# A selective-scan stage on one core: the per-chunk front work placed three steps earlier, and exponentials four states ahead instead of three

## The chip, the core and the metric

The kernel runs on 1 core of one Trainium2 chip. The metric is the device time of one execution in microseconds (us). All of it is one launch; nothing is computed on the host.

The core has five engines with a queue each, and each works its queue strictly in the order of the program: PE (TensorE, matmuls), DVE (VectorE), ACT (ScalarE), POOL (GpSimd) and SP (SyncE, which here only issues DMAs). An instruction that waits for a semaphore holds up everything behind it on its engine.

## What is computed

The reference is four layers on x of shape (8, 128, 64, 64), each of the form `x = x + layer(group_norm(x))`. The change touches layer 0 alone, so only that is shown, cut to what matters (D = 64, DI = 128, N = 16 states, L = 4096 positions, 8 images):

```python
x_id, x_hw = x[:, :64], x[:, 64:]                 # two halves of the channels
t  = (tokens(x_id) @ expand_w) @ concat_w + concat_b
xs, z = split(layer_norm(t) @ in_w + in_b)        # 2 x 128
xc = silu(conv1d_3(xs))                           # 3 causal taps
dt, Bm, Cm = softplus(xc @ ... ), xc @ ..., xc @ ...
h_t = exp(dt_t * A) * h_(t-1) + dt_t * Bm_t * xc_t     # for each of 16 states
y_t = sum_n h_t[n] * Cm_t[n] + xc_t * D
x_id_out = t + (y * silu(z)) @ out_w + out_b
hw = conv3x3(x_hw)
x = x + relu(concat(x_id_out, hw))
```

Layers 1 to 3 (a row and column propagation, a gated convolution, a deformable convolution) follow and are the same in both kernels.

## The kernel before, in words

Layer 0 is the function `layer0`. Its work is cut into 64 **chunks** of 512 positions: 8 chunks (`NCH`) of each of 8 images. Channels lie on the 128 partitions, positions along the free dimension, so every tile is 128x512. Image 0 is unrolled, images 1 to 7 are one hardware loop.

A chunk g has 16 **steps** n = 0 to 15, one for each state. Each engine runs its own list of steps, and semaphores tie the lists together:

- DVE (L1007, L1017, L999): *product* n+1 (dt*x times the B row, in PSUM), then *scan* n (the recurrence over 512 positions). So a chunk begins with products 0 and 1 and then scan 0. After scan 2 comes *gated* of the chunk before: it reads the finished sum `pY` and multiplies it by silu(z).
- POOL (L979): *weigh* n, h times the C row, after scan n, into one of eight buffers `hc`.
- PE: at step n first *spread* n+3 (L884; it broadcasts the B row of that state into one of four PSUM banks `pB`, after scan n-1; from n = 13 on these are spreads 0, 1, 2 of the next chunk), then the *sums* (L873; sum k adds the weighed state k into `pY` after weigh k). `SUM_AT` says which at which step: 11 at step 13, 12 at step 14, 13 at step 15, and, as `LATE_SUM_AT`, 14 and 15 at steps 0 and 1 of the next chunk. Then the 3x3 convolution's matmuls that `CONV_AT` gives to the step (`taps`: first the direct one, L890, which waits until `fin` of the chunk before has been read out of `pO`; then two low ones, L893, on partitions 64 to 127; then three pairs, L896).
- ACT (L940): *decay*, the exponential exp(dt*A) of the state `LEAD` ahead of n; at step 3 also the *direct term* (L928, xc*D into `pY`, which must wait for gated and comes before sum 0), at step 4 the *result* (L933, relu into `fin`), at step 13 the statistics.

Beside that, each chunk has **front work**, which is done for a chunk ahead: norm, halo, centre, variance, deviation, normalise (which make `un`), taps and gate input (the causal conv and z), silu (xc and silu(z), with a table load before and after), projections, dt argument, round B and C (whose last write is `c_out`), log, rest of B and C, softplus (two instructions), dt, dt * x. Three tables `PE_AT`, `ACT_AT` and `POOL_AT` put each at the end of a step. On POOL a chunk has 16 weighs, one result addition (L984, step 6) and six front instructions, 23 in all. SP loads inputs and the broadcast C rows; its own list isn't changed.

A matmul on fp32 data shows in the trace as two records ("x2"); a spread is one. Two matmuls that use different partition halves (a low convolution tap beside centre or variance, tap 2 beside the gate input) run side by side.

Of the kernel before, what the change touches and what calls it, by code (L numbers as in the profile page):

```python
# [24 lines left out]
B, H, W = 8, 64, 64  # L25
HW = H * W
CH = 512
NCH = HW // CH
ROWS = CH // W
HALF = 64  # L30
NS = 16
# [8 lines left out]
def after(eng, sem, k, lag=0):  # L40


    eng.wait_ge(sem, k + (1 + CREDIT - lag))
# [456 lines left out]
def layer0(nc, G, x_dram, x1_dram, c_dram):  # L500
# [3 lines left out]
    NDA = 8  # L504
    NHC = 8
    NB = 4
    LEAD = 3
    KEEP = G.KEEP
    with ExitStack() as ctx:
        def sb(name, shape, dt=F32):  # L510
            return ctx.enter_context(nc.sbuf_tensor(name, shape, dt))
# [24 lines left out]
        rest = sb("m_rest", [P, CH])  # L536
# [3 lines left out]
        dt = sb("m_dtv", [P, 2, CH])  # L540
# [21 lines left out]
        def sem(name):  # L562
# [20 lines left out]
        s.passed = ctx.enter_context(nc.semaphore("m_waits_passed"))  # L583


        PE_AT = {0: ["tap 0"], 1: ["tap 1"], 2: ["tap 2", "gate input"], 5: ["project B, C", "project dt"], 8: ["centre"],
                 10: ["variance"]}
        ACT_AT = {1: ["norm", "halo"], 3: ["silu"], 6: ["dt argument", "round B, C"], 8: ["log", "pad"], 9: ["centre"],
                  11: ["deviation"]}
        POOL_AT = {7: ["rest of B, C"], 9: ["softplus"], 10: ["dt"], 11: ["dt * x"], 13: ["normalise"]}  # L590
        TWO_AHEAD = ("norm", "halo", "centre", "variance", "deviation", "normalise")
        CONV_AT = {7: 1, 8: 1, 10: 1, 11: 1, 13: 1, 15: 1}
        SUM_AT = {4: (0, 1), 6: (2, 3), 7: (4, 5), 8: (6,), 9: (7,), 10: (8,), 11: (9,), 12: (10,), 13: (11,), 14: (12,),
                  15: (13,)}
        LATE_SUM_AT = {0: 14, 1: 15}
# [117 lines left out]
        def front_pool(g, b, c, what):  # L713
            pool, par = nc.gpsimd, c % 2
            if what == "normalise":
                after(pool, s.rstd, g)
                after(pool, s.z, g, 2)
                after(pool, s.cv, g, 2)
                after(pool, s.halo, g, 1)
                pool.tensor_tensor(un[:, par, 2:2 + CH], tc[:], sq[:], ALU.mult).then_inc(s.u, 1)  # L720
            if what == "rest of B, C":
                after(pool, s.c_out, g)
                after(pool, s.HC, NS * (g - 1) + 7)
                pool.tensor_tensor(bcs[32:64, par, :], bcf[32:64, par, :], bcs[32:64, par, :].bitcast(F32),
                                   ALU.subtract).then_inc(s.blo, 1)
                after(pool, s.blo, g)
            if what == "softplus":
                after(pool, s.r1, g)
                pool.tensor_tensor(rest[:], ea[:], rest[:], ALU.subtract).then_inc(s.r2, 1)
                after(pool, s.r2, g)  # L730
                after(pool, s.ln, g)
                pool.tensor_tensor(rest[:], rest[:], ln[:], ALU.add).then_inc(s.r3, 1)
            if what == "dt":
                after(pool, s.r3, g)
                after(pool, s.xb, g)
                pool.tensor_tensor(dt[:, par, :], dt[:, par, :], rest[:], ALU.add).then_inc(s.dt, 1)  # L736
            if what == "dt * x":
                after(pool, s.dt, g)
                after(pool, s.xc, g)
                after(pool, s.U, 16 * g - 16, 1)  # L740
                pool.tensor_tensor(dtx[:, par, :], dt[:, par, :], xc[:, par, :], ALU.mult).then_inc(s.dtx, 1)

        def program(eng, at, chunk, front, finish, before=lambda: None):

            def parts(n, one_ahead, two_ahead):
                for what in at.get(n, ()):
                    where = two_ahead if what in TWO_AHEAD else one_ahead
                    if where:  # L750
                        front(*where, what)

            def image(b, last):
                def place(c):

                    if c >= NCH:
                        return b * NCH + c, (b + 1) % B, c - NCH
                    return b * NCH + c, b, c
                for c in range(NCH):
                    prev = place(c - 1) if c else (b * NCH - 1, b - 1, NCH - 1) if last else None  # L760
                    chunk(b * NCH + c, b, c, prev, lambda n: parts(n, place(c + 1), place(c + 2)))
            for n in range(NS):
                parts(n, None, (0, 0, 0))
            for n in range(NS):
                parts(n, (0, 0, 0), (1, 0, 1))
            before()
            image(0, False)
            with eng.Fori(1, B) as b:
                image(b, True)
            finish(B * NCH - 1, B - 1, NCH - 1)  # L770

        with nc.Block() as block:
            @block.sync
            def _(sp):
# [82 lines left out]
                after(sp, s.sum, NS * G_LAST + NS - 1)  # L857
                after(sp, s.dA, NS * B * NCH + LEAD - 1)
                for b in range(KEEP, G.NI):
# [8 lines left out]
            def _(pe):  # L868
                def sum_state(g, n):
                    after(pe, s.HC, NS * g + n)  # L870
                    if n == 0:
                        after(pe, s.dterm, g)
                    pe.matmul(pY[:], G.ident, hc[:, n % NHC, :], start=False, stop=(n == NS - 1),  # L873
                              skip_group_check=True).then_inc(s.sum, 1)
# [5 lines left out]
                def spread_B(g, n, par):  # L880
                    if n == 0:
                        after(pe, s.blo, g)
                    after(pe, s.S, NS * g + n, NB)
                    pe.matmul(pB[:, n % NB, :], T.pick[:, n:n + 1].to_broadcast([P, P]), bcs[:, par, :],  # L884
                              start=True, stop=True).then_inc(s.B, 1)
# [12 lines left out]
                def chunk(g, b, c, prev, parts_ahead):  # L898
                    tap = taps(g, c)
                    for n in range(NS):  # L900
# [8 lines left out]
                        for k in SUM_AT.get(n, ()):  # L909
                            sum_state(g, k)  # L910
                        for _ in range(CONV_AT.get(n, 0)):
                            next(tap)
                        parts_ahead(n)

                def finish(g, b, c):
                    for k in LATE_SUM_AT.values():
                        sum_state(g, k)
                    project_out(g, c)
                pe.matmul(pY[:], G.ident, G.small[:, 0:CH], start=True, stop=True).then_inc(s.border, 1)
                program(pe, PE_AT, chunk, front_pe, finish, lambda: [spread_B(0, n, 0) for n in range(3)])  # L920

            @block.scalar
            def _(act):
# [28 lines left out]
                def chunk(g, b, c, prev, parts_ahead):  # L952
                    for n in range(NS):
                        if n < NS - LEAD:
                            decay(g, n + LEAD, c % 2)
                        else:
                            decay(g + 1, n + LEAD - NS, 1 - c % 2)
                        if n == 3:
# [7 lines left out]
                def finish(g, b, c):  # L966
                    result(g, b, c)
                    statistics(g, b, c)
                program(act, ACT_AT, chunk, front_act, finish, lambda: [decay(0, n, 0) for n in range(LEAD)])

            @block.gpsimd
            def _(pool):
# [13 lines left out]
                def chunk(g, b, c, prev, parts_ahead):  # L986
                    for n in range(NS):
# [3 lines left out]
                        parts_ahead(n)  # L991
                program(pool, POOL_AT, chunk, front_pool, result)

# [865 lines left out]
```

## Time and profile before

| | us |
|---|---|
| median of 3 runs (7603.76 to 7632.84) | 7619.43 |
| the profiled execution's span | 7648.3 |
| layer 0: first to last *gated*, 64 of them | 141.0 to 2121.3 |
| PE busy, whole span | 5717.8 (75%) |
| DVE busy | 5490.3 (72%) |
| POOL busy | 4111.0 (54%) |
| ACT busy | 3409.0 (45%) |

The profiled execution took 29 us (0.4%) more than the median. Layer 0 is 26% of the span. Shares over the whole span mix four layers with different limits, so layer 0 is read chunk by chunk, in the timeline of each engine. In that timeline one row is an instruction or a run of equal ones; the start of the next row is the truer measure of what an instruction costs its engine, since the recorded lengths overlap by some hundredths of a microsecond.

### The profile page before, as it was taken

The numbers are of one execution on the slowest core, as the hardware profiler recorded it, in microseconds if no ns is written. First come the engines' busy times: TensorE is split into PE (matmuls) and PEld (weight loads), VectorE is DVE, ScalarE is ACT, GpSimd is POOL, SyncE is SP. The second block draws the span as 40 slices with busy tenths as digits, with TensorE's granted clock in tenths as the row PEclk, the third lists the DMA queues.
The fourth block names the chain that finished last, engine by engine and source line by source line (L and its number), as shares of the span: only waits on it lengthen the run. The fifth ranks groups of instructions, "written<-read, shape, count | busy, mean of one in ns | idle before, by whom it ended". The sixth has DMA issues, their size and how long they took to land. (4 is left out here: it accounts for less than half of the span.)

```text
span 7648.3 us, 89071 instructions
## 1 busy us (share of the span) xinstructions
PE 5717.8 (75%) x21147; PEld 3269.1 (43%) x21147; DVE 5490.3 (72%) x12779; ACT 3409.0 (45%) x7221; POOL 4111.0 (54%) x3871
## 2 busy tenths in 40 slices
PE   5999999999989999999865565655656565565442
PEld 2444444444478888888532222322223232232111
DVE  6999999999967777778565666556566665665556
ACT  4888888888855211111233333333333333333333
POOL 4999999999910001000055555655556565565663
PEclk9999999999999999999987676877778777687665
DMA  5445444444420000000156555555555665555567
GB/s 193 170 179 180 167 169 172 170 168 167 168 87 3 3 0 23 0 0 0 42 164 198 164 184 178 168 183 168 180 180 172 193 184 183 178 176 179 178 182 265
DMA packets 306397, 1093.60 MB, mean 143 GB/s; under 512 B 56560, under 2 KB 58639, under 8 KB 264604
## 3 DMA queue, kind: packets, MB, share of 16 engines
q0 software_dynamic: 187440, 625.23, 27.1%
q1 hardware_dynamic: 118516, 464.08, 17.0%
q14 instruction: 359, 2.94, 0.1%
q8 instruction: 82, 1.34, 0.1%
HBM read 997.72 MB, written 91.37 MB: 142 GB/s over the span
## 5 line engine op out<-in xcount | busy, mean ns | idle before, releaser
L1281 POOL DMA_INDIRECT d_ring<-corner_table,d_idx_now x2304 | 2212.2, 960 | 1635.9 <-issue 950.2
L1481 PE MATMUL d_ps_s<-small,d_mix 128*128 128x128 f32 x2304 | 489.6, 350 | 1544.2 <-DVE d_mix L1653 1010.5
L979 POOL TENSOR_TENSOR X<-X 128x512 f32<-128x512 f32 x1024 | 1289.7, 1277 | 168.3 <-DVE X L1017 150.9
L1481 PEld LDWEIGHTS d_ps_s<-small,d_mix 128*128 128x128 f32 x2304 | 327.8, 176 | 2071.0 <-issue 1089.5
L1653 DVE SCALAR_TENSOR_TENSOR d_acc<-d_ring,d_w_now,d_mix 128x128 f32<-128x128 f32 x2304 | 660.9, 354 | 694.3 <-ACT d_mix L1327 321.5
L1017 DVE TENSOR_TENSOR_SCAN X<-X,m_pB 128x512 f32<-128x512 f32 x896 | 1132.4, 1269 | 0.0
L873 PE MATMUL m_pY<-X,small 128*128 128x512 f32 x2048 | 1040.4, 605 | 90.3 <-POOL X L979 90.2
L277 PE MATMUL prop_ps<-prop_parts,prop_w_hi 128*128 128x480 f32 (+4 forms) x4536 | 1099.8, 387 | 4.6 <-DVE prop_parts L286 4.6
L1327 ACT ACTIVATE d_mix<-d_ring,d_w_now 128x128 f32<-128x128 f32 x2304 | 732.3, 390 | 719.1 <-DMA d_ring<-corner_table,d_idx_now 659.1
L277 PEld LDWEIGHTS prop_ps<-prop_parts,prop_w_hi 128*128 128x128 f32 x4536 | 816.0, 188 | 133.4 <-DVE prop_parts L286 5.4
L1411 PE MATMUL d_ps_out<-d_samp,d_dcn_w 128*128 128x512 f32 x1152 | 832.0, 815 | 7.9 <-ACT X L1314 5.8
L1007 DVE TENSOR_TENSOR m_pB<-m_dtx,m_pB 128x512 f32<-128x512 f32 x1024 | 693.0, 678 | 92.2 <-PE m_pB L884 69.3
L884 PE MATMUL m_pB<-m_bcs,m_pick 128*128 128x512 f32 x1027 | 758.9, 739 | 0.1
L940 ACT ACTIVATE X<-m_dtv,m_A 128x512 f32<-128x512 f32 x1027 | 688.5, 713 | 96.3 <-POOL m_dtv L736 74.7
L225 ACT ACTIVATE prop_sum<-prop_ps 128x256 f32<-128x256 f32 x504 | 194.5, 386 | 1169.4 <-PE prop_ps L277 1169.4
L1653 DVE SCALAR_TENSOR_TENSOR d_mix<-d_ring,d_w_now,d_acc 128x128 f32<-128x128 f32 x2304 | 646.8, 340 | 85.1 <-remote 45.7
L1653 DVE SCALAR_TENSOR_TENSOR d_acc<-d_ring,d_w_now,d_acc 128x128 f32<-128x128 f32 x2304 | 649.5, 348 | 43.5 <-DVE d_acc L1653 26.4
L272 PEld LDWEIGHTS prop_ps<-prop_parts,prop_w_lo 128*128 128x128 f32 x4536 | 598.3, 189 | 51.8 <-issue 9.8
L272 PE MATMUL prop_ps<-prop_parts,prop_w_lo 128*128 128x240 f32 (+4 forms) x4536 | 604.1, 277 | 16.4 <-POOL prop_w_lo L200 9.6
L873 PEld LDWEIGHTS m_pY<-X,small 128*128 128x128 f32 x2048 | 363.7, 188 | 469.8 <-POOL X L979 281.6
L1440 PE MATMUL l_ps_a<-l_xn,l_w 128*128 128x512 f32 x896 | 462.9, 648 | 24.1 <-DVE l_gate L1541 24.1
L200 POOL TENSOR_TENSOR prop_w_lo<-prop_raw,prop_w_hi 128x1152 fp32r<-128x1152 f32 x4 | 10.6, 2648 | 793.1 <-ACT prop_w_hi L218 793.1
(231 smaller groups left out, 7744.8 us busy)
## 6 DMA issues: line engine op xcount, KB each, us to landing
X<-c_scratch SPq DMA_DIRECT2D x256, 1024.0 KB, 4.9
d_ring<-corner_table,d_idx_now POOLq DMA_INDIRECT x2304
corner_table<-d_tT SPq DMA_DIRECT2D x120, 256.0 KB
X<-in_x SPq DMA_DIRECT2D x8, 2048.0 KB, 15.2
m_res<-in_x SPq DMA_DIRECT2D x64, 256.0 KB, 4.6
x_scratch<-m_res SPq DMA_DIRECT2D x64, 256.0 KB, 2.1
x_scratch<-X SPq DMA_DIRECT2D x8, 2048.0 KB
b_x<-x_scratch POOLq DMA_DIRECT2D x16, 1024.0 KB, 11.7
```

What stands on the lines that cost most here:

```text
L272: pe.matmul(ps[s][:, 1, a:b, :], w_lo[:, d % 2, k * P:(k + 1) * P], parts[s][:, 0, a + k - MID:b + k - MID, :], start=(k == MID), stop=Fal ...
L277: mm = pe.matmul(ps[s][:, :, a:b, :], w_hi[:, d % 2, k * P:(k + 1) * P], parts[s][:, :, a + k - MID:b + k - MID, :], start=False, stop=(k ...
L873: pe.matmul(pY[:], G.ident, hc[:, n % NHC, :], start=False, stop=(n == NS - 1), skip_group_check=True).then_inc(s.sum, 1)
L884: pe.matmul(pB[:, n % NB, :], T.pick[:, n:n + 1].to_broadcast([P, P]), bcs[:, par, :], start=True, stop=True).then_inc(s.B, 1)
L979: pool.tensor_tensor(hc[:, n % NHC, :], h[:, n, :], Cb[:, n, :], ALU.mult).then_inc(s.HC, 1)
L1007: dve.tensor_tensor(pB[:, n % NB, :], dtx[:, c % 2, :], pB[:, n % NB, :], ALU.mult).then_inc(s.U, 1)
L1017: dve.tensor_tensor_scan(h[:, n, :], dA[:, n % NDA, :], pB[:, n % NB, :], T.zero[:, 0:1] if c == 0 else h[:, n, CH - 1:CH], ALU.mult, ALU. ...
L1281: pool.indirect_dma_start(out=ring[:, m % RING, :], out_offset=None, in_=flat, in_offset=bass.IndirectOffsetOnAxis(ap=idx_now[:, c % 2, m: ...
L1327: r0 = act.activation(R[:, k % 3, t, :], ring[:, m % RING, 0:P], ACT.Copy, scale=w_now[:, c % 2, 4 * m:4 * m + 1])
L1411: pe.matmul(ps_out[:], dcn_w[:, k, :], samp[:, k % 3, :], start=(k == 0), stop=(k == TAPS - 1)).then_inc(s_dcn, 1)
L1481: turned = pe.transpose(ps_s[k % 3][:, t, :], R[:, k % 3, t, :], G.ident)
L1653: mixed = dve.scalar_tensor_tensor(R[:, k % 3, t, :] if corner == 3 else acc[:, t, :], ring[:, m % RING, corner * P:(corner + 1) * P], w_n ...
```

## The change

The front work moves three steps earlier on all engines: what stood at step n of a chunk for the next chunk stands at n-3 now, and what falls off the beginning goes to the end of the chunk before, one chunk further ahead (three tables with the distance written beside each name, `AHEAD = 3` passes before the first chunk instead of two). "pad" stays at step 8. The convolution's direct tap and first low tap move to step 5, the others to 7, 9, 10 and 12. `LEAD` is 4. Sums, the result additions, the direct term and the statistics stay where they were.

```diff
-    LEAD = 3
+    LEAD = 4
-        PE_AT = {0: ["tap 0"], 1: ["tap 1"], 2: ["tap 2", "gate input"], 5: ["project B, C", "project dt"], 8: ["centre"],
-                 10: ["variance"]}
-        ACT_AT = {1: ["norm", "halo"], 3: ["silu"], 6: ["dt argument", "round B, C"], 8: ["log", "pad"], 9: ["centre"],
-                  11: ["deviation"]}
-        POOL_AT = {7: ["rest of B, C"], 9: ["softplus"], 10: ["dt"], 11: ["dt * x"], 13: ["normalise"]}
-        TWO_AHEAD = ("norm", "halo", "centre", "variance", "deviation", "normalise")
-        CONV_AT = {7: 1, 8: 1, 10: 1, 11: 1, 13: 1, 15: 1}
+        PE_AT = {2: [("project B, C", 1), ("project dt", 1)], 5: [("centre", 2)], 7: [("variance", 2)],
+                 13: [("tap 0", 2)], 14: [("tap 1", 2)], 15: [("tap 2", 2), ("gate input", 2)]}
+        ACT_AT = {0: [("silu", 1)], 3: [("dt argument", 1), ("round B, C", 1)], 5: [("log", 1)], 6: [("centre", 2)],
+                  8: [("pad", 1), ("deviation", 2)], 14: [("norm", 3), ("halo", 3)]}
+        POOL_AT = {4: [("rest of B, C", 1)], 6: [("softplus", 1)], 7: [("dt", 1)], 8: [("dt * x", 1)],
+                   10: [("normalise", 2)]}
+        AHEAD = 3
+        CONV_AT = {5: 2, 7: 1, 9: 1, 10: 1, 12: 1}
...
-                after(pool, s.HC, NS * (g - 1) + 7)
+                after(pool, s.HC, NS * (g - 1) + 4)
...
-            for n in range(NS):
-                parts(n, None, (0, 0, 0))
-            for n in range(NS):
-                parts(n, (0, 0, 0), (1, 0, 1))
+            for g in range(-AHEAD, 0):
+                for n in range(NS):
+                    parts(n, lambda ahead: (g + ahead, 0, g + ahead) if g + ahead >= 0 else None)
```

**POOL, a chunk of image 0.** L979 is weigh, L984 the result, L724 rest of B and C, L729 and L732 softplus, L736 dt, L741 dt * x, L720 normalise. Before, from the nine weighs 14, 15, 0 to 6 on:

```order
L979 TENSOR_TENSOR X<-X 128x512 x9
L984 TENSOR_TENSOR m_res<-m_res,m_fin 128x512
L979 TENSOR_TENSOR X<-X 128x512
L724 TENSOR_TENSOR m_bcs<-m_bcf,m_bcs 32x512
L979 TENSOR_TENSOR X<-X 128x512 x2
L729 TENSOR_TENSOR m_rest<-m_ea,m_rest 128x512
L732 TENSOR_TENSOR m_rest<-m_rest,m_ln 128x512
L979 TENSOR_TENSOR X<-X 128x512
L736 TENSOR_TENSOR m_dtv<-m_dtv,m_rest 128x512
L979 TENSOR_TENSOR X<-X 128x512
L741 TENSOR_TENSOR m_dtx<-m_dtv,m_xc 128x512
L979 TENSOR_TENSOR X<-X 128x512 x2
```

The same place now, from the ten weighs 11 to 15 and 0 to 4 on (front lines have moved by one line number):

```order
L979 TENSOR_TENSOR X<-X 128x512 x10
L725 TENSOR_TENSOR m_bcs<-m_bcf,m_bcs 32x512
L979 TENSOR_TENSOR X<-X 128x512 x2
L984 TENSOR_TENSOR m_res<-m_res,m_fin 128x512
L730 TENSOR_TENSOR m_rest<-m_ea,m_rest 128x512
L733 TENSOR_TENSOR m_rest<-m_rest,m_ln 128x512
L979 TENSOR_TENSOR X<-X 128x512
L737 TENSOR_TENSOR m_dtv<-m_dtv,m_rest 128x512
L979 TENSOR_TENSOR X<-X 128x512
L742 TENSOR_TENSOR m_dtx<-m_dtv,m_xc 128x512
L979 TENSOR_TENSOR X<-X 128x512 x2
L721 TENSOR_TENSOR m_un<-m_tc,m_sq 128x512
```

All seven instructions that aren't weighs stand between weigh 4 and weigh 11 now; before they stood between weigh 6 and weigh 14.

**PE, from step 13 to step 1 of the next chunk**, image 0. L873 is a sum, L884 a spread, L896 a convolution pair, L614 a causal tap. Before, from sum 11 to sum 15:

```order
L873 MATMUL m_pY<-X,small 128x512
L896 MATMUL m_pO<-m_xn,m_pairs 128x512
L884 MATMUL m_pB<-m_bcs,m_pick 128x512
L873 MATMUL m_pY<-X,small 128x512
L884 MATMUL m_pB<-m_bcs,m_pick 128x512
L873 MATMUL m_pY<-X,small 128x512
L896 MATMUL m_pO<-m_xn,m_pairs 128x512
L884 MATMUL m_pB<-m_bcs,m_pick 128x512
L873 MATMUL m_pY<-X,small 128x512
L614 MATMUL m_pf0<-m_un,m_scan_in 128x512
L884 MATMUL m_pB<-m_bcs,m_pick 128x512
L873 MATMUL m_pY<-X,small 128x512
```

The same place now, again from sum 11 to sum 14:

```order
L873 MATMUL m_pY<-X,small 128x512
L615 MATMUL m_pf0<-m_un,m_scan_in 128x512
L884 MATMUL m_pB<-m_bcs,m_pick 128x512
L873 MATMUL m_pY<-X,small 128x512
L615 MATMUL m_pf0<-m_un,m_scan_in 128x512
L884 MATMUL m_pB<-m_bcs,m_pick 128x512
L873 MATMUL m_pY<-X,small 128x512
L615 MATMUL m_pf0<-m_un,m_scan_in 128x512
L621 MATMUL m_pf1<-m_un,m_inz 128x512
L884 MATMUL m_pB<-m_bcs,m_pick 128x512
L873 MATMUL m_pY<-X,small 128x512
```

Between sum 11 and sum 15 stood four spreads, sums 12 to 14, two pairs and one tap; now four spreads, the same sums, and the three taps with the gate input beside the last. One spread and sum 15 follow.

**ACT, around the direct term (L928)**, image 0. Before:

```order
L928 ACTIVATE m_pY<-m_xc,m_D 128x512
L685 ACT_TABLE_LOAD
L685 ACTIVATE m_xc<-m_pf,m_scan_b 128x512
L688 ACTIVATE m_sz<-m_pf,m_in_b 128x512
L689 ACT_TABLE_LOAD
L940 ACTIVATE X<-m_dtv,m_A 128x512
L933 ACTIVATE m_fin<-m_pO,m_finb 128x512
```

Now:

```order
L686 ACTIVATE m_xc<-m_pf,m_scan_b 128x512
L689 ACTIVATE m_sz<-m_pf,m_in_b 128x512
L690 ACT_TABLE_LOAD
L940 ACTIVATE X<-m_dtv,m_A 128x512 x3
L928 ACTIVATE m_pY<-m_xc,m_D 128x512
L694 ACTIVATE m_ea<-m_pf,m_dtb 128x512
L696 ACTIVATE m_dtv<-m_pf,m_dtb 128x512
L698 ACTIVATE m_ea<-m_ea 128x512
L702 ACTIVATE m_bcs<-m_pf 128x512
L705 ACTIVATE m_bcf<-m_pf 80x512
L940 ACTIVATE X<-m_dtv,m_A 128x512
L933 ACTIVATE m_fin<-m_pO,m_finb 128x512
```

The silu pair stands ahead of the direct term now, and five instructions of the dt argument and of round B, C have come between the direct term and the result `fin`. On PE the direct tap, which waits for `fin`, stands at step 5 instead of step 7.

## Rows read from the trace of the kernel before

**Rows 1.** Windows: busy us of each engine in one chunk, then clock, DMA:

```profile
1013.08:1044.54 31.46, 29.88 (x79) 12.76 (x78) 29.33 (x33) 25.78 (x44) 28.63 (x24) 1.00 0.49 168
```

**Rows 2.** All of gated (L999): duration, first and last start, idle before:

```profile
L999 DVE TENSOR_TENSOR m_sz<-m_pY,m_sz x64: 662/692/693, 141.0 to 2121.3; 128x512 f32<-128x512 f32 x64
...
  PE m_pY L873: 88.2, 58
```

**Rows 3.** Timeline, DVE (start, length, name, idle before): gated, scans, the chunk's boundary:

```profile
1021.14 0.69 DVE L999 TENSOR_TENSOR m_sz<-m_pY,m_sz 128x512 f32<-128x512 f32 x1 [1.44 <-PE m_pY L873]
...
1024.12 1.27 DVE L1017 TENSOR_TENSOR_SCAN X<-X,m_pB 128x512 f32<-128x512 f32 x1
...
1044.54 0.69 DVE L1007 TENSOR_TENSOR m_pB<-m_dtx,m_pB 128x512 f32<-128x512 f32 x1 [0.29 <-POOL m_dtx L741]
1045.58 0.70 DVE L1007 TENSOR_TENSOR m_pB<-m_dtx,m_pB 128x512 f32<-128x512 f32 x1 [0.34 <-PE m_pB L884]
...
1052.60 0.69 DVE L999 TENSOR_TENSOR m_sz<-m_pY,m_sz 128x512 f32<-128x512 f32 x1 [1.45 <-PE m_pY L873]
```

**Rows 4.** Timeline, POOL, from weigh 4 to the run of weighs 14, 15, 0, 1, 2:

```profile
1025.54 1.28 POOL L979 TENSOR_TENSOR X<-X 128x512 f32<-128x512 f32 x1 [0.50 <-DVE X L1017]
...
1029.08 1.27 POOL L979 TENSOR_TENSOR X<-X 128x512 f32<-128x512 f32 x1 [0.50 <-DVE X L1017]
...
1031.54 1.29 POOL L979 TENSOR_TENSOR X<-X 128x512 f32<-128x512 f32 x1
1032.97 1.27 POOL L724 TENSOR_TENSOR m_bcs<-m_bcf,m_bcs 32x512 fp32r<-32x512 f32 x1
1034.49 2.51 POOL L979 TENSOR_TENSOR X<-X 128x512 f32<-128x512 f32 x2 [0.25 <-PE m_pY L873]
1036.97 1.26 POOL L729 TENSOR_TENSOR m_rest<-m_ea,m_rest 128x512 f32<-128x512 f32 x1
1038.31 1.27 POOL L732 TENSOR_TENSOR m_rest<-m_rest,m_ln 128x512 f32<-128x512 f32 x1
...
1048.15 6.20 POOL L979 TENSOR_TENSOR X<-X 128x512 f32<-128x512 f32 x5
```

**Rows 5.** Timeline, PE, from sum 11 at the chunk's boundary on:

```profile
1043.33 1.12 PE L873 MATMUL m_pY<-X,small 128*128 128x512 f32 x2 [1.08 <-POOL X L979]
1044.29 1.02 PE L896 MATMUL m_pO<-m_xn,m_pairs 128*128 128x512 f32 x2
...
1049.49 1.12 PE L873 MATMUL m_pY<-X,small 128*128 128x512 f32 x2 [0.25 <-POOL X L979]
1050.45 1.02 PE L614 MATMUL m_pf<-m_un,m_scan_in 128*128 128x512 f32 x2
...
1051.54 1.02 PE L873 MATMUL m_pY<-X,small 128*128 128x512 f32 x2
1052.40 1.02 PE L614 MATMUL m_pf<-m_un,m_scan_in 128*128 128x512 f32 x2
...
1053.59 0.69 PE L614 MATMUL m_pf<-m_un,m_scan_in 64*128 64x512 f32 x1
...
1054.98 1.02 PE L878 MATMUL m_pO<-m_sz,m_out 128*128 128x512 f32 x2
```

**Rows 6.** Timeline, ACT, silu to the decay behind its load; dt argument; round B, C:

```profile
1023.87 0.69 ACT L685 ACTIVATE m_xc<-m_pf,m_scan_b 128x512 f32<-128x512 f32 x1
...
1026.45 0.72 ACT L940 ACTIVATE X<-m_dtv,m_A 128x512 f32<-128x512 f32 x1
...
1028.88 0.67 ACT L693 ACTIVATE m_ea<-m_pf,m_dtb 128x512 f32<-128x512 f32 x1
...
1031.02 0.59 ACT L704 ACTIVATE m_bcf<-m_pf 80x512 f32<-80x512 f32 x1
```

**Rows 7.** Timeline before the first chunk: DVE's products 0 and 1, PE's taps:

```profile
105.07 1.29 DVE L1007 TENSOR_TENSOR m_pB<-m_dtx,m_pB 128x512 f32<-128x512 f32 x2 [40.59 <-PE m_pB L884]
...
107.10 2.08 PE L614 MATMUL m_pf<-m_un,m_scan_in 128*128 128x512 f32 x2 [0.79 <-POOL m_un L720]
```

More of the change, by code:

```diff
@@ L743, in program, with parts @@
         def program(eng, at, chunk, front, finish, before=lambda: None):
-            def parts(n, one_ahead, two_ahead):
-                for what in at.get(n, ()):
-                    where = two_ahead if what in TWO_AHEAD else one_ahead
+            def parts(n, place):
+                for what, ahead in at.get(n, ()):
+                    where = place(ahead)
                     if where:
@@ L760, in image @@
                     prev = place(c - 1) if c else (b * NCH - 1, b - 1, NCH - 1) if last else None
-                    chunk(b * NCH + c, b, c, prev, lambda n: parts(n, place(c + 1), place(c + 2)))
-            for n in range(NS):
-                parts(n, None, (0, 0, 0))
-            for n in range(NS):
-                parts(n, (0, 0, 0), (1, 0, 1))
+                    chunk(b * NCH + c, b, c, prev, lambda n: parts(n, lambda ahead: place(c + ahead)))
+            for g in range(-AHEAD, 0):
+                for n in range(NS):
+                    parts(n, lambda ahead: (g + ahead, 0, g + ahead) if g + ahead >= 0 else None)
             before()
```

## The prediction

> **What bounds the kernel now.** I first looked at the windows, one chunk long, because the page's shares mix four layers. In one chunk of 31.46 us DVE is busy 29.33, POOL 28.63, ACT 25.78 [rows 1]. Nothing is busy all the time, so a chunk is set by a loop of waits and not by one engine. The 64 gated instructions start from 141.0 to 2121.3 [rows 2], which is 63 periods of 31.43 us: the chunk shown is typical, and all that follows is a sum over one period, times 63.
>
> Then DVE's timeline, for where it is idle. Per chunk it waits 0.29 for dt * x, 0.34 for spread 1 and 1.44 for the finished sum before gated [rows 3]; over the layer the last comes to 88.2 us in 58 places [rows 2]. Without any of these a chunk takes DVE some 29.1 to 29.4. Gated waits for sum 15, sum 15 stands on PE behind sum 14, and sum 14 (1049.49) waits for POOL's weigh 14, which starts at 1048.15 and ends 1.27 later [rows 4, 5].
>
> Then I followed POOL backward. From weigh 4 to weigh 6 it waits 0.5 us for DVE before each [rows 4]; from weigh 6 to weigh 14 it is never idle for lack of a scan, since seven front or result instructions stand between these weighs. So the loop is: gated, scans 3 and 4 (1024.12), weigh 4 (1025.54): 4.40 us; two more scans to weigh 6 (1029.08): 3.54; weigh 6 to the end of weigh 14: 1048.15 + 1.27 - 1029.08 = 20.34; to sum 14: 0.07; sum 14 to gated (1052.60): 3.11. Sum 31.46, the period itself [rows 3 to 5]. This is the loop that binds.
>
> **The change, part by part.**
>
> *POOL.* It has the same 23 instructions, but the seven between weighs now stand between weigh 4 and weigh 11. POOL falls behind DVE from weigh 4 on and no longer at weigh 6. What happens next is decided by which weigh PE waits for. Weigh n follows weigh n-1 every 1.23 us (five in 6.20, of which the last is 1.27 long); the rest of B and C starts 1.43 after the weigh before it and the weigh behind it 1.52 later; the second softplus instruction starts 1.34 after the first [rows 4]. The 0.25 beside the 1.52 names a sum that had long been done; I take it as the cost of POOL's wait for its own write, which moves with the instruction. From the start of weigh 4 to the end of weigh 11 there are now 15 instructions: 1.43 + 1.52 + 1.34 + 11 x 1.23 + 1.27 = 19.09.
>
> *PE.* The three taps and the gate input now stand between sums 11 and 15, where two convolution pairs and one tap stood. That is nearly the same work; what differs is where PE is released. Run without a wait, from rows 5: a sum after a wait 0.96 (1043.33 to 1044.29), a matmul 0.86 (1051.54 to 1052.40), a matmul and a spread 1.09 (1050.45 to 1051.54), tap 2 beside the gate input with its spread 1.39 (1053.59 to 1054.98), the last sum 1.02 long. Sum 11, tap 0 + spread, sum 12, tap 1 + spread, sum 13, taps + spread, sum 14 + spread, sum 15: 0.96 + 1.09 + 0.86 + 1.09 + 0.86 + 1.39 + 1.09 + 1.02 = 8.36, and 0.04 to gated.
>
> *The new loop.* Gated to weigh 4 is 4.40 as before (DVE's list isn't touched). Then 19.09 to the end of weigh 11, 0.05 to sum 11, 8.40 to gated: **31.94 us**. Against the old loop it gives up one POOL instruction (-1.25) and two scans (-3.54) and takes in 5.3 us more of PE's queue. The other loops through the same queues are shorter, and this decides that weigh 11 is the one: through weigh 15, 19.09 + 4 x 1.23 + 4.40 + 0.05 + 1.06 = 29.5; through weigh 10 (two instructions earlier, then sum 10, a convolution pair and spread 0) 31.4. PE must also have reached sum 11 in time, which I work out next.
>
> *The direct tap and ACT.* The direct tap used to find `fin` long read. Now `fin` comes behind the silu pair, three decays, the direct term and five instructions. Count from sum 11. Taps end at 4.86 + 1.12 = 5.98; silu to the decay behind its load takes 2.58 (1023.87 to 1026.45), three decays 1.95, the direct term 0.61, dt argument to the end of `c_out` 1031.02 + 0.59 - 1028.88 = 2.73 [rows 6]: `c_out` at 13.9, `fin` after one decay and one relu at 15.1. PE, with sums 14 and 15, two projections, the output projection, sums 0 and 1 and their spreads, comes to the direct tap at 13.4, so it waits 1.7 us there, a wait that the trace doesn't have. What hides it is PE's slack: its 28 matmul slots and 16 spreads need 28.7 of 32. From 15.1 to sum 11 of the next chunk PE has the direct tap (0.96), two low taps in pairs with their spreads (2.8), 12 more matmuls (10.3) and six spreads (1.4), 15.5 in all, and on the way it waits about 1 us for weighs 8 to 10: it is there at some 31.6, weigh 11 ends at 31.9, so the cover is 0.3 us. It does cost DVE: spread 11 stands behind sums 2 to 5 and the low tap, and arrives some 1.2 us late. That delays the end of the chunk on DVE, but product 1 of the next waits for a spread behind sum 11 anyway, so it isn't added. POOL needs `c_out` at 8.40 + 4.40 + 1.43 = 14.2 from sum 11, 0.3 after it is there.
>
> *LEAD 4* costs nothing: it is the same number of decays, and DVE never waited for one; ACT has 6 us free per chunk. *The dt * x wait* of 0.29 [rows 3] goes, since dt * x is done before weigh 9, but product 1 behind it waits for PE in either kernel: worth 0. *SP*: `c_out` comes at most some 5 us earlier, the C rows are stored and loaded sooner or at the same time: 0.
>
> *Small waits.* Two covers are 0.3 us and the gated instruction comes only 0.2 behind DVE's own arrival. Whatever fails of these adds and nothing of it subtracts: bounds 0 to 0.2 us per chunk. I take 0.06, nearer to zero because the old loop closes to 0.01 us without any. Period 32.0.
>
> *The start.* Before, product 0 of the first chunk started at 105.07 and the second chunk's taps only at 107.10, after normalise [rows 7]. Now these taps stand ahead of spread 0. One tap is 2.08 long there, against 1.02 in the middle of the layer [rows 5, 7], since PE has just begun to be busy. At 1.5 to 1.8 us for each of the three taps and one spread behind them, some 5.3 us pass: product 0 at 112.4, +7.3. The tail gains 0.3.
>
> *Sum.* 63 x (32.0 - 31.46) = 34.0, + 7.3 + 0.3 = 41.6. On the profiled execution's 7648.3 this gives 7690; on the median of the runs, 29 us below it with the same kernel, **7661**. That is 0.55% more. About 0.5%, 38 us, is what a measurement of this kernel can tell from no change.
>
> **Rivals.**
>
> *Faster: the sums are ready earlier.* The last weigh of a chunk ends 5 us behind the last scan and not 6.4, so sum 15 and gated could come earlier. If weigh 15 were the release, the period would be 29.5: 63 x -1.94 + 7.6 = -115, 7505. For it speaks the 1.44 us wait before gated, which is fed by exactly these weighs. Against it: sum 15 stands in a queue behind sums 11 to 14 and the taps, and PE has to run 8.36 us after weigh 11 whatever weigh 15 does. This is also where a rule of the Trainium skill points (Perfetto Trace Analysis, Optimization Strategy): find the gaps of the most contended engine, see which semaphore they wait for, and make these dependencies start sooner. By occupancy that engine is DVE, and the front does start sooner here; by that rule the time would be this rival's 7505. The rows of POOL and PE speak against it, as the dependency that DVE waits for becomes ready later at weigh 11 although earlier at weigh 15. Chance 0.12.
>
> *No change: weigh 11 isn't late enough.* If POOL reaches weigh 11 half a microsecond earlier than by my sum (say the 1.52 behind the rest of B and C shrinks to 1.23 and a weigh overlaps more), the loop through weigh 10 or the old period holds: 31.4 to 31.5, and only the start remains: 7619 + 7 = 7627. Chance 0.18.
>
> *Slower by more: ACT is late.* `c_out` is ready 0.3 us before POOL asks for it. If silu's start, a table load or a decay slips by more than that, POOL waits in the middle of the binding loop, and every further 0.1 us costs 6.3 us. At 0.5 us beyond the margin: 63 x 0.5 = 32 more, 7693. Chance 0.15.
>
> *It doesn't do what it says*, that is, the order stays as it was: excluded by the order of the instructions.
>
> **How the numbers follow.** Forecast 0.55, from 7640 to 7685 by its small terms; about two thirds of it is beyond 0.5%. With the no-change rival: faster 0.12, same 0.18 + 0.19 = 0.37, slower 0.36 + 0.15 = 0.51. The range leaves out the fast rival and the last of the slow one: 7605 to 7705.
>
> **What would show it.** In a chunk of the changed kernel: a period near 32.0; sum 11 waiting for its weigh, and no POOL wait at sums 12 to 15; POOL without idle time from weigh 4 to the weighs of the next chunk; the direct tap waiting some 1.7 us for ACT; product 11 on DVE waiting about 1.2 us, product 1 about 0.5, gated hardly 0.2. The first chunk starts 7 us later. Wrong would be: gated closer than 8 us behind sum 11, POOL waiting for scans behind weigh 4, or `c_out` later than the weigh before it.

## The result, and the profile after

The changed kernel takes 7668.44 us (median of 4 runs, 7639.43 to 7683.83), the kernel before 7612.83 beside it. The ratio is 1.0066, 95% interval 1.0038 to 1.0094: slower by 0.7%. The forecast was 7661 and slower by 0.55%, counted from 7619.43.

The profiled execution has a span of 7681.7 us. The groups that answer to [rows 2], all gated of the changed kernel and what they waited for:

```profile
L999 DVE TENSOR_TENSOR m_sz<-m_pY,m_sz x64: 691/692/693, 146.6 to 2174.2; 128x512 f32<-128x512 f32 x64
...
  PE m_pY L873: 7.9, 8
```

The first gated starts 5.5 us later than before, the last 52.9 us later, so the 63 periods between them take 2027.7 us instead of 1980.3: 47.4 more. The wait of gated has almost gone (7.9 us, 8 times, against 88.2 and 58), and yet each period is longer. This profiled span grew by only 33.4 us, since the layers behind were 19.5 us shorter in this execution; the medians grew by 55.6. Layer 0 is the part that can be read to a tenth of a microsecond, and from here on I compare its periods.

One chunk of the changed kernel by windows, as [rows 1]:

```profile
660.41:692.51 32.10, 30.14 (x79) 12.75 (x78) 29.47 (x34) 24.98 (x42) 28.65 (x23) 1.00 0.51 175
```

The engines do what they did (PE 30.14, DVE 29.47, POOL 28.65); the chunk is 0.64 longer. DVE's timeline of that chunk, as [rows 3], has its waits elsewhere: products 11, 1 and 3 wait for their spreads, and gated has no wait of its own in the list:

```profile
660.41 0.69 DVE L999 TENSOR_TENSOR m_sz<-m_pY,m_sz 128x512 f32<-128x512 f32 x1
...
663.39 1.27 DVE L1017 TENSOR_TENSOR_SCAN X<-X,m_pB 128x512 f32<-128x512 f32 x1
...
674.85 0.69 DVE L1007 TENSOR_TENSOR m_pB<-m_dtx,m_pB 128x512 f32<-128x512 f32 x1 [1.33 <-PE m_pB L884]
...
686.26 0.69 DVE L1007 TENSOR_TENSOR m_pB<-m_dtx,m_pB 128x512 f32<-128x512 f32 x1 [0.69 <-PE m_pB L884]
...
690.55 0.70 DVE L1007 TENSOR_TENSOR m_pB<-m_dtx,m_pB 128x512 f32<-128x512 f32 x1 [0.47 <-PE m_pB L884]
...
692.51 0.69 DVE L999 TENSOR_TENSOR m_sz<-m_pY,m_sz 128x512 f32<-128x512 f32 x1
```

POOL's timeline, as [rows 4], from weigh 4 (the last with a wait for a scan) to the run of weighs 11 to 15 and 0:

```profile
664.82 1.28 POOL L979 TENSOR_TENSOR X<-X 128x512 f32<-128x512 f32 x1 [0.50 <-DVE X L1017]
666.24 1.27 POOL L725 TENSOR_TENSOR m_bcs<-m_bcf,m_bcs 32x512 fp32r<-32x512 f32 x1
667.74 2.51 POOL L979 TENSOR_TENSOR X<-X 128x512 f32<-128x512 f32 x2 [0.23 <-POOL m_bcs L725]
...
681.46 1.26 POOL L721 TENSOR_TENSOR m_un<-m_tc,m_sq 128x512 f32<-128x512 f32 x1
682.68 7.41 POOL L979 TENSOR_TENSOR X<-X 128x512 f32<-128x512 f32 x6
```

And PE's, as [rows 5], from sum 11 (684.00, behind weigh 11, which ends at 683.95) to sum 15 (691.45), plus the direct tap of the same chunk:

```profile
667.04 1.12 PE L890 MATMUL m_pO<-m_xnc,m_direct 128*128 128x512 f32 x2 [1.45 <-ACT m_fin L933]
...
684.00 1.12 PE L873 MATMUL m_pY<-X,small 128*128 128x512 f32 x2 [0.25 <-POOL X L979]
684.97 1.02 PE L615 MATMUL m_pf<-m_un,m_scan_in 128*128 128x512 f32 x2
...
688.01 1.02 PE L873 MATMUL m_pY<-X,small 128*128 128x512 f32 x2
688.96 0.69 PE L615 MATMUL m_pf<-m_un,m_scan_in 64*128 64x512 f32 x1
...
691.45 1.02 PE L873 MATMUL m_pY<-X,small 128*128 128x512 f32 x2
```

Gated still hangs on sum 15, by a little: it starts 0.04 behind the end of sum 15 (691.45 + 1.02), and 1.35 behind the start of scan 2 (691.16), where an instruction that needn't wait comes 1.19 behind a scan's start. DVE and PE arrive 0.16 us apart, and product 3, which DVE waits for just before, needs a spread of the same stretch on PE.

So the loop that was forecast can be read off: gated to weigh 4 4.41 (660.41 to 664.82); weigh 4 to the end of weigh 11 19.13 (682.68 + 1.27); 0.05 to sum 11; sum 11 to gated 8.51. Sum 32.10. Forecast were 4.40, 19.09, 0.05 and 8.40.

The periods are not all alike. Between two gated, the 56 periods of images 1 to 7 are 32.05 to 32.10 in most places, 32.15 once per image, 32.34 once per image, and 33.02 to 33.04 once per image, at its first chunk (885.30 to 918.34 in the trace); in image 0 they are 31.83. The 33.02 can be traced to the rows of the first chunk of an image, ACT and then POOL:

```profile
882.95 1.28 ACT L686 ACT_TABLE_LOAD   x1 [3.80 <-PE m_pf L615]
884.25 0.69 ACT L686 ACTIVATE m_xc<-m_pf,m_scan_b 128x512 f32<-128x512 f32 x1
```

```profile
889.71 1.27 POOL L979 TENSOR_TENSOR X<-X 128x512 f32<-128x512 f32 x1 [0.50 <-DVE X L1017]
892.10 1.26 POOL L725 TENSOR_TENSOR m_bcs<-m_bcf,m_bcs 32x512 fp32r<-32x512 f32 x1 [1.12 <-ACT m_bcf L705]
```

In the chunks between these the table load in front of silu is done while ACT waits for the taps, as here:

```profile
684.20 1.28 ACT L686 ACT_TABLE_LOAD   x1
690.12 0.69 ACT L686 ACTIVATE m_xc<-m_pf,m_scan_b 128x512 f32<-128x512 f32 x1 [4.64 <-PE m_pf L615]
```

At the first step of the hardware loop's body it stands behind that wait, so silu starts 1.30 us behind the load's start instead of at once, all behind it is as much later, `c_out` misses its 0.3 us of cover, and POOL waits 1.12 us inside the loop that binds.

### The profile page after: what moved, and what is told of

Its sections match the earlier page's. It is cut to its first block and busy times, and to the rows that moved or that the text cites. A ratio compares the mean times of both kernels' runs of the same rounds, so it can differ in the third digit from the quotient of the medians.

```text
span 7681.7 us, 89086 instructions
## 1 busy us (share of the span) xinstructions
PE 5695.6 (74%) x21155; PEld 3254.2 (42%) x21155; DVE 5506.1 (72%) x12779; ACT 3401.5 (44%) x7224; POOL 4115.0 (54%) x3871
## 5 line engine op out<-in xcount | busy, mean ns | idle before, releaser
L979 POOL TENSOR_TENSOR X<-X 128x512 f32<-128x512 f32 x1024 | 1286.7, 1276 | 213.4 <-DVE X L1017 124.6
L873 PE MATMUL m_pY<-X,small 128*128 128x512 f32 x2048 | 1039.9, 605 | 39.2 <-POOL X L979 31.4
L884 PE MATMUL m_pB<-m_bcs,m_pick 128*128 128x512 f32 x1027 | 750.7, 732 | 3.1 <-DVE X L1017 3.1
L873 PEld LDWEIGHTS m_pY<-X,small 128*128 128x128 f32 x2048 | 365.7, 189 | 391.9 <-POOL X L979 207.0
```

What stands on the lines that cost most here:

```text
L979: pool.tensor_tensor(hc[:, n % NHC, :], h[:, n, :], Cb[:, n, :], ALU.mult).then_inc(s.HC, 1)
```

## The experiments

For each kernel, on one profiled execution: layer 0 from first to last gated, the usual period of images 1 to 7; and the ratio to the kernel before, timed on the same chip, with its 95% interval.

| kernel | layer 0, us | period, us | ratio to before |
|---|---|---|---|
| before | 1980.3 | 31.45 | 1 |
| changed | 2027.7 | 32.08 | 1.0066 (1.0038 to 1.0094) |
| changed, again | 2026.8 | 32.06 | 1.008 (1.0065 to 1.0096) |
| a_pool_op_9 | 2089.4 | 33.06 | 1.0139 (1.0091 to 1.0188) |
| a_pool_op_12 | 2027.9 | 32.09 | 1.007 (1.0042 to 1.0099) |
| a_tap0_twice | 2081.8 | 32.94 | 1.0151 (1.0102 to 1.0199) |
| a_proj_twice | 2027.7 | 32.08 | 1.0055 (1.003 to 1.0079) |
| a_fin_sooner | 2027.8 | 32.08 | 1.007 (1.0055 to 1.0086) |
| a_lead3 | 2027.9 | 32.09 | 1.0074 (1.0059 to 1.009) |
| a_norm11 | 2005.8 | 31.56 | 1.004 (1.0024 to 1.0055) |
| a_cout_sooner | 2020.3 | 32.07 | 1.0069 (1.0054 to 1.0084) |
| b_norm14 | 1950.1 | 30.92 | 0.9958 (0.9944 to 0.9972) |
| b_norm14_res5 | 1936.3 | 30.40 | 0.9937 (0.9924 to 0.9951) |
| b_norm14_res5_conv12 | 1924.7 | 30.20 | 0.9921 (0.9907 to 0.9934) |

Not all ran on one chip. The kernel before took 7621 us on the chip of a_pool_op_9, a_pool_op_12, a_tap0_twice and a_proj_twice, 6890 on that of a_fin_sooner, a_lead3, a_norm11 and b_norm14, and 6880 on that of the other four. Layer 0 took the same time on each (the changed kernel 2027.7 and 2026.8), so the periods compare across chips and the medians don't.

**One more POOL instruction, inside and outside the loop.** My theory is that the loop through weigh 4, weigh 11, sum 11 and gated sets the period. The same instruction is put at two places, four instructions apart on POOL.

```diff
 def chunk(g, b, c, prev, parts_ahead):      # on POOL
     for n in range(NS):
         weigh(g, n)
...
+        if n == 9:                          # a_pool_op_9; 12 in a_pool_op_12
+            pool.tensor_tensor(filler[:], G.small[:, 0:CH], G.small[:, 0:CH], ALU.mult)
         parts_ahead(n)
```

> The changed kernel with one more POOL instruction per chunk (a 128x512 multiply into a tile that nobody reads, on data that nobody writes) at step 9, that is, between weigh 9 and weigh 10. Weigh-11 loop (my theory): gated to weigh 4, weigh 4 to weigh 11, sum 11 to gated binds, so an instruction inside it costs its full 1.23 us: period 32.1 to 33.3, layer 0 +78 us over the changed kernel, some 7746 us in all. Rival, the wait for fin on PE and the late product 11 are what costs: POOL has 3 us free per chunk and PE would sooner wait for fin than for a weigh, so at most 0.3 us per chunk, +20 us.

> The same instruction at step 12, behind weigh 12 and ahead of weigh 13, thus outside the weigh-11 loop but inside a loop through weigh 15 (31.0 us with it). Weigh-11 loop: 0, period stays 32.1, within 3 us of the changed kernel in layer 0. Rival, the last weigh releases gated (the faster rival of the prediction), or POOL's load as such counts: +1.23 us per chunk, +78 us, the same as at step 9.

At step 9 the period grew by 0.98 and layer 0 by 61.7 us; at step 12 by 0.01 and 0.2 us. The instruction reads one tile twice and costs 1.00 us there and not 1.23, from its start to the next weigh's:

```profile
1029.80 1.04 POOL L993 TENSOR_TENSOR m_filler<-small 128x512 f32<-128x512 f32 x1
1030.80 1.28 POOL L980 TENSOR_TENSOR X<-X 128x512 f32<-128x512 f32 x1
```

So its whole length counts in one place and nothing of it three steps later. I had its price too high by 0.23, and the place right. This also rules out that the end of POOL's chunk (weigh 15) or POOL's load as such sets the time, which was the faster rival of the prediction turned round.

**One more matmul on PE, inside and outside.** A matmul is issued twice; the second writes the same values over the first.

```diff
-                rows = slice(0, HALF if j == 2 else P)                       # a_tap0_twice: within "if j == 0:"
+                    pe.matmul(pf[0][:], T.scan_in[:, 0, :], un[:, par, 0:CH], start=True, stop=True)
+                rows = slice(0, HALF if j == 2 else P)
...
             if what == "project B, C":                                       # a_proj_twice
                 after(pe, s.xc, g)
+                pe.matmul(pf[0][:], T.bc[:], xc[:, par, :], start=True, stop=True)
                 pe.matmul(pf[0][:], T.bc[:], xc[:, par, :], start=True, stop=True).then_inc(s.bc, 1)
```

> The changed kernel with tap 0 issued twice (the second overwrites the first, same result), so one more matmul on PE between sum 11 and sum 15. Weigh-11 loop: the stretch from sum 11 to gated is part of it and runs without a wait, so +0.86 us per chunk: period 32.9 to 33.0, +55 us, some 7723 us. Rival, POOL alone or DVE sets the period: PE has 3 us free per chunk, so 0.

> The changed kernel with the projection of B and C issued twice (same result), one more matmul on PE at step 2, ahead of the direct tap's 1.44 us wait for fin. Weigh-11 loop: that wait hides 0.86 us, and the stretch from gated to sum 11 has the slack: 0, period stays 32.1 (at most +0.1, if the second projection makes the dt argument late). The wait of the direct tap shrinks to some 0.6 us. Rival, PE's total work sets the period wherever it stands: +0.86 us per chunk, +55 us, the same as with tap 0 twice.

Between sum 11 and sum 15 it costs 0.86 per period, 54.1 us in layer 0. At step 2 it costs nothing, and the direct tap's wait takes it up. The longest waits of PE and DVE from 500 to 1500 us (total, times, longest) of a_proj_twice:

```profile
DVE m_pB L1008 <- PE m_pB L885: 74.2, 92, 1.3
...
PE m_pO L891 <- ACT m_fin L934: 27.3, 31, 1.6
```

and of the changed kernel:

```profile
DVE m_pB L1007 <- PE m_pB L884: 77.3, 93, 1.3
...
PE m_pO L890 <- ACT m_fin L933: 46.2, 31, 1.6
```

The wait for `fin` falls from 1.49 to 0.88 us in the mean. PE is busy 30.14 of 32.10 us and has spare time all the same, but none of it between sum 11 and gated.

**The new waits as a cause.** The most visible new things in the profile are the direct tap's 1.45 us for `fin` and product 11's 1.33. The rival is that these are the price.

```diff
 def chunk(g, b, c, prev, parts_ahead):      # on ACT, a_fin_sooner
...
-        if prev and n == 4:
-            result(*prev)
         if prev and n == 13:
             statistics(*prev)
         parts_ahead(n)
+        if prev and n == 3:
+            result(*prev)
```

> The changed kernel with ACT's result (fin) at the end of step 3, ahead of the next decay instead of behind it, so 0.6 us sooner; everything else the same. Weigh-11 loop: the direct tap's wait shrinks from 1.44 to about 0.8 us and product 11's on DVE from 1.33 to about 0.7, and the period stays 32.1: 0. Rival, the new waits for fin and at product 11 are what made the change slower: period shorter by up to 0.6, -38 us.

```profile
DVE m_pB L1007 <- PE m_pB L884: 72.9, 116, 1.3
...
PE m_pO L890 <- ACT m_fin L933: 27.2, 31, 1.0
```

The direct tap waits 0.88 instead of 1.49, and the period stays 32.08, layer 0 within 0.1 us. DVE's waits for spreads shift among themselves (72.9 us in 116 waits against 77.3 in 93): product 11 waits 0.72 instead of 1.33, but product 14, which didn't wait, now waits 0.42 for a spread that stands on PE behind weigh 8's sum, and product 1 waits 0.76 instead of 0.69. The rival is out: both waits shrank by 0.6 us and the period didn't move.

**The lead of the exponentials.** a_lead3 is the changed kernel with `LEAD = 3`.

> The changed kernel with the exponentials three states ahead again (LEAD 3), the rest of the change kept. My theory: the lead plays no part in the period, 0; but with one decay fewer ahead of the direct term nothing moves, as only their order around silu changes; ACT's chain from silu to the end of round B, C still has three decays in it. Rival, the longer lead is what makes fin and the last conversion late: shorter wait at the direct tap and a shorter period.

2027.9 against 2027.7 us. With the rest of the change in place, that part is worth nothing in either direction.

**The missed cover at an image's first chunk.**

```diff
-                  3: [("dt argument", 1), ("round B, C", 1)], ...
+                  3: [("round B, C", 1), ("dt argument", 1)], ...
```

> The changed kernel with round B, C ahead of the dt argument on ACT's step 3, so that its last write c_out comes 1.7 us sooner. In 7 of the 63 periods, at the first chunk of an image, POOL waits 1.1 us for c_out and the period is 33.0 instead of 32.1. If that wait is the whole of the 0.95, these periods fall to 32.1 and layer 0 loses 6 to 7 us; the other periods stay at 32.08 (the dt argument isn't on the loop). Rival, the image's first chunk costs 0.95 for another reason (loop branch): 33.0 stays.

The seven periods of 33.02 became 32.07 and nothing else moved; layer 0 went from 2026.8 (the changed kernel on the same chip) to 2020.3. POOL's wait for `c_out` is no longer among its waits. The 0.95 is that wait and no more. Why the table load stands behind ACT's wait there, and in front of it elsewhere, no run tells. The medians (6926.56 and 6935.29) show the same 9 us at the edge of what they can tell.

**Taking one instruction out of the loop.** In the changed kernel POOL's normalise goes behind weigh 11; in the kernel before, behind weigh 14, where its own loop ended:

```diff
-                   10: [("normalise", 2)]}         # a_norm11
+                   11: [("normalise", 2)]}
...
-        POOL_AT = {..., 13: ["normalise"]}         # b_norm14
+        POOL_AT = {..., 14: ["normalise"]}
```

> The changed kernel with POOL's normalise at step 11 instead of 10, behind weigh 11. Weigh-11 loop: weigh 11 ends 1.23 sooner; then the loop through weigh 10, sum 10, a convolution pair and spread 0 takes over at 4.42 + 16.67 + 0.05 + 2.05 + 8.40 = 31.6. Period 31.6, -30 us against the changed kernel, about that of before. Rival, POOL's total or PE's total binds: no change. Rival, tap 0 then waits for normalise and becomes the end of the loop: its sum is 31.1, so no.

> The kernel before with POOL's normalise at step 14 instead of 13, behind weigh 14. If the old loop is gated, weigh 6, weigh 14, sum 14, gated (31.46 us), weigh 14 ends 1.23 sooner and the loop through weigh 13 takes over: 7.94 to weigh 6, 17.88 to the end of weigh 13, 0.05, sum 13, a pair and spread 3 2.06, sum 14 to gated 3.01: 30.94. Period 30.9, -33 us against the kernel before, 0.4%, so some 7580 us. Rival, DVE's waits at the chunk's start bind by themselves: no change. Rival, tap 0 waits longer for normalise than weigh 14 gains: slower.

a_norm11: period 31.56, forecast 31.6. b_norm14: 30.92, forecast 30.94, and faster than the kernel before by 0.42%. One of b_norm14's chunks:

```profile
1005.71 0.69 DVE L999 TENSOR_TENSOR m_sz<-m_pY,m_sz 128x512 f32<-128x512 f32 x1 [0.93 <-PE m_pY L873]
...
1036.63 0.69 DVE L999 TENSOR_TENSOR m_sz<-m_pY,m_sz 128x512 f32<-128x512 f32 x1 [0.93 <-PE m_pY L873]
```

Layer 0 of a_norm11 shrank by only 21.9 us, not the 33 that 0.52 per period make, since six periods, where the hardware loop goes from one image to the next, are 33.9 to 34.6 long; the ones behind them fell from 33.0 to 31.5. More on that below.

**A version that beats both.** From b_norm14, POOL's result addition goes to step 5, where POOL still idles 0.5 us before each weigh, and then the last convolution pair on PE goes from step 15 to step 12, out of the stretch between sum 13 and gated:

```diff
-                        if prev and n == 6:        # POOL, b_norm14_res5
+                        if prev and n == 5:
                             result(*prev)
...
-        CONV_AT = {7: 1, 8: 1, 10: 1, 11: 1, 13: 1, 15: 1}      # and b_norm14_res5_conv12
+        CONV_AT = {7: 1, 8: 1, 10: 1, 11: 1, 12: 1, 13: 1}
```

> The kernel before with normalise at step 14 and the result addition on POOL at step 5 instead of 6, where POOL still waits 0.5 us for each scan. The loop through weigh 13 (30.94) then enters POOL's busy stretch at weigh 5 with 6.18 + 2.46 = 8.64 us to weigh 6's end of wait instead of 7.94 + 1.23 = 9.17, so -0.53: period 30.4, -34 us against the version with normalise alone and -67 us against the kernel before (0.9% to 1%). Rival, something else binds behind the 30.9, DVE's own waits at the chunk's start or PE: period stays 30.9.

> The same and the last convolution pair on PE at step 12 instead of 15, out of the stretch between sum 13 and gated. The loop through weigh 13 drops to 29.6; next is weigh 14, normalise, tap 0 (which waits for it), spread, sum 15, gated: 7.41 + 20.39 + 2.15 = 29.95. DVE's own floor is 29.1 to 29.4. Period 30.0, -93 us against the kernel before (1.2% to 1.35%). Rival, PE's queue is late at spread 0 or at sum 11 with the pair at step 12, so product 1 comes later: period 30.4 or more.

Periods 30.40 and 30.20. The first is as forecast; the second is 0.2 above its 29.95 to 30.0. The rival for it, that PE's queue comes late, isn't borne out. These are the rows of one of its chunks from gated to gated, with PE's weight loads (PEld), where a wait of PE's queue is seen:

```profile
991.13 0.69 DVE L999 TENSOR_TENSOR m_sz<-m_pY,m_sz 128x512 f32<-128x512 f32 x1 [0.85 <-PE m_pY L873]
997.31 1.27 POOL L979 TENSOR_TENSOR X<-X 128x512 f32<-128x512 f32 x1 [0.49 <-DVE X L1017]
...
1017.61 1.26 POOL L720 TENSOR_TENSOR m_un<-m_tc,m_sq 128x512 f32<-128x512 f32 x1
1018.84 4.95 POOL L979 TENSOR_TENSOR X<-X 128x512 f32<-128x512 f32 x4
...
1018.92 0.30 PEld L614 LDWEIGHTS m_pf<-m_un,m_scan_in 128*128 128x128 f32 x2 [0.92 <-POOL m_un L720]
...
1020.15 0.30 PEld L873 LDWEIGHTS m_pY<-X,small 128*128 128x128 f32 x2 [0.50 <-POOL X L979]
...
1021.32 0.69 DVE L999 TENSOR_TENSOR m_sz<-m_pY,m_sz 128x512 f32<-128x512 f32 x1 [0.81 <-PE m_pY L873]
```

Tap 0 (L614, 1018.92) starts 0.05 behind normalise (L720) and sum 15 (L873, 1020.15) as closely behind weigh 15, the first of the four, so PE waits for POOL. The loop is the one that was forecast for this version: gated to weigh 5 6.18, weigh 5 to the end of normalise 21.56, from there through tap 0 and sum 15 to gated 2.45; sum 30.19. The forecast had 27.80 for the first two together (measured 27.74) and 2.15 for the last. That is 1.09 from tap 0 to sum 15 and 1.06 from sum 15 to gated, PE's prices without a wait. Here these are 1.23 and 1.17, and 0.05 goes by before tap 0 starts. Sum 15 also waits for weigh 15, which ends some 0.04 before it, so a loop through weigh 15 is as long as this one, and the two can't be told apart.

The gain of whole runs, 0.63% and 0.79%, is below the 0.9% and 1.2% that were forecast, because of the turns of the hardware loop: in both, six periods are about 34 us long, 3.5 to 4.1 more than the others.

## Why the prediction was right, point by point

- **What bounds before.** The loop through weigh 6, weigh 14, sum 14 and gated was added up to 31.46 and tested by b_norm14: one POOL instruction moved out of it, the period fell by 0.53 to the next loop in line, 30.92 against 30.94 worked out. The row of [rows 1] also has PE busy for 29.88 us, more than any other engine, which the prediction leaves out; a_proj_twice shows that this isn't a limit by itself.
- **The new loop.** 31.94 was forecast, 32.0 with small waits; measured 32.08. Its pieces are above: 0.01, 0.04 and 0.11 more than forecast. The 0.11 is on PE: tap 2 beside the gate input starts 0.95 behind sum 13 (688.01 to 688.96), where I had 0.86. The rows of before could have told: a tap and a spread in front of the half-size tap 2 take 1.19 there (1052.40 to 1053.59 in [rows 5]), and I had priced the same place without these 0.1. The 0.25 that POOL idles behind the rest of B and C was taken for a wait for its own write; the changed kernel's trace names it so (0.23, for `m_bcs` from POOL). That the loop binds, and that it leaves POOL at one of weighs 10 to 12 and runs on PE between sums 11 and 15, is shown by the two pairs of added instructions: full price inside, nothing outside. That it is weigh 11, a_norm11 shows: an instruction moved from in front of it to behind it shortened the period. The neighbour through weigh 10 was put at 31.4; worked out again it is 31.6, and a_norm11 has 31.56.
- **The direct tap's wait for `fin`.** Forecast 1.7 us, hidden; measured 1.45 and hidden (a_proj_twice, a_fin_sooner). Product 11's wait: 1.2 forecast, 1.33 measured; product 1's 0.5 and 0.69.
- **LEAD 4**: forecast 0, measured 0.2 us of 2028.
- **The start.** Forecast +7.3, measured +5.5: product 0 of the first chunk starts at 110.62 instead of 105.07 [rows 7]. Normalise came 1.4 us sooner than I had assumed (the taps start at 105.70 and not at 107.10), and the three taps with their spread took 4.9 us and not 5.3. The changed kernel's second run has product 0 at 112.01, so this term is known to 1.4 us at best, and its size proves little.
- **The sum.** Layer 0: 41.6 us forecast (34.0 in the periods, 7.6 at the ends), 52.9 measured. The 11 us between them: 6.6 are seven times the 0.95 at an image's first chunk; some 1.9 are seven times 0.27, in one chunk per image, where the weigh behind the rest of B and C starts 1.79 and not 1.5 after it, for a reason that I don't know; some 5.0 are the 0.08 by which the usual period is above 32.0; the start takes 1.8 off. What is left is below half a microsecond. The old period was taken as 31.46 for all 63, while those of image 0 are 31.2; the new ones of image 0 are 31.83 and not 32.08, and the two nearly cancel.
- **Luck.** The median came out 7 us above the forecast. That is closer than the sum deserves, since its base was the median of three runs, 7619.43, and four gave 7612.83: a growth of 41.6 us was forecast, and 55.6 was measured in the medians.
- **The term that was too small** is "small waits", 0.06 per period. The 63 periods are 32.19 in the mean, 0.25 above the 31.94 of the loop. Of this 0.16 are pieces of the loop, PE's above all, that were priced too low in every period, some 0.14 are real waits in 14 of the 63, and the shorter periods of image 0 take some 0.04 off. The prediction had the right place for the larger of these (`c_out` with 0.3 us of cover, and a table load or silu that slips), and gave the whole of it to a rival, 0.15 likely, for all chunks; it comes true in 7 of 63. What I missed is that one chunk in eight isn't like the others: I had read `c_out`'s cover in one chunk and not at the loop's turn.
- **The faster rival** fell: weigh 15 does end sooner after its scan than before and gated's wait did vanish, and the period grew all the same. The rule of the Trainium skill that I had put beside it (Perfetto Trace Analysis, Optimization Strategy: make what the most contended engine waits for start sooner) isn't contradicted, but the trace shows what it needs here. DVE's wait was for sum 15, and in the changed kernel sum 15 hangs on weigh 11. The change made that later: weigh 11 ends 23.5 us behind gated (683.95 - 660.41) and before some 22.1 (sum 11, which starts right behind it, at 1043.33 with gated at 1021.14).

## What to carry to other kernels

Where every engine still waits somewhere, write down the loop that binds, as a sum of rows from one instruction to the same instruction a period later, and check that it adds up to the period. Then cost a change of order by what it puts into that loop and what it takes out, and work out the loops next in line, since the gain ends there. The largest visible waits don't tell what it costs: here the one that vanished (1.44 us before gated) made nothing faster, and the two that appeared (1.45 and 1.33) could be made 0.6 shorter without any gain.

Moving work earlier on an engine helps only if it moves in front of the stretch that binds. Here it put all seven of POOL's front and result instructions ahead of weigh 11, where PE then had three taps to run before the sum that mattered.

Read one turn of the hardware loop as well as one period in its middle.

## What the runs showed of the hardware

- **The turn of the hardware loop.** The loop goes from one image to the next six times. DVE's first product after the turn is late by very different times. At the first turn DVE idles 0.87 us in the changed kernel run again and 1.42 in b_norm14, but 3.69 in a_norm11 and 3.83 in b_norm14_res5, with the same instructions on DVE as in the kernel that each was made from. The last scans of an image and the first products of the next, in b_norm14_res5:

```profile
586.82 2.44 DVE L1017 TENSOR_TENSOR_SCAN X<-X,m_pB 128x512 f32<-128x512 f32 x2
593.09 1.29 DVE L1007 TENSOR_TENSOR m_pB<-m_dtx,m_pB 128x512 f32<-128x512 f32 x2 [3.83 <-PE m_pB L884]
```

The spread that is named had been done for over 3 us. ACT stands still for 2.79 us at the same turn, until 591.96, with nothing named. A load of C rows was issued at 586.47 and landed 5.1 us later; from 588 to 590 the DMA engines were 95% busy with it. The trace has DMA queues that it calls "instruction". They moved one packet from 586 to 588, none from 588 to 590, four from 590 to 592 and three from 592 to 594, just as ACT and DVE go on. That fits engines that wait at the turn for their instructions behind that load. No run moves the load, so it isn't shown. The long turns cost the fastest version some 23 us of layer 0.
- **Chips differ.** The kernel before took 7613 to 7621 us on some and 6880 to 6890 on others, while layer 0 of the changed kernel took 2027.7 us on a slower and 2026.8 on a faster one. The whole difference is in the layers that gather by DMA. In the changed kernel the first gather is issued at 3890.6 on the slower chip and 3890.7 on the faster, the last at 7582.3 and 6832.8: 749.5 us apart, and the spans differ by 749.1. From 4000 to 6800 us DMA moved 181 GB/s on the one and 227 on the other.
- **The place of a table load** relative to a wait changes at the loop's first step, which moved a chain of a dozen ACT instructions by 1.3 us once per image.
